# Attention stacks filled during the q, k, v stage of a transformer layer on one Trainium2 core

## What is computed

```
x = x + 0.5 * ffn(layernorm(x))
x = x + attn(layernorm(x))          # recurrent, 2 heads of 64
x = x + 0.5 * ffn(layernorm(x))

def ffn(x):                          # 16 heads of 8 channels, 8 experts
    x = x + msa(layernorm(x, ln1))
    return x + moe(layernorm(x, ln2))

def msa(x):
    q, k, v = split(x @ w_qkv)       # per batch and head: 512 x 8 each
    attn = softmax(q @ k.T / sqrt(8))
    return (attn @ v) @ w_proj
```

## Time and profile before

| | us |
|---|---|
| median of the timed runs (3) | 1562.1 |
| lowest and highest of them | 1561.02, 1567.3 |
| the profiled execution | 1553.92 |
| its span | 1552.0 |

### The profile page before, as it was taken

One profiled execution on the slowest core, in us unless ns is written; L12 is line 12 of the kernel. 1 busy time (PEld: TensorE's weight loads), 2 busy tenths in 40 slices (PEclk: granted clock), 3 DMA queues, 4 the chain that ended last, 5 costly groups with the idle time before them and its releaser, 6 DMA issues. The chain is left out here.

```text
span 1552.0 us, 39914 instructions
## 1 busy us (share of the span) xinstructions
PE 1284.2 (83%) x12720; PEld 729.3 (47%) x12721; DVE 1082.9 (70%) x1864; ACT 859.3 (55%) x1750; POOL 659.1 (42%) x767
## 2 busy tenths in 40 slices
PE   5499999999978595288789747499999999976693
PEld 3244444444368595135445444234444444376693
DVE  8588888888555233668788758688888888464232
ACT  3178888888831352234334414178888888820451
POOL 4323333333337463355566533323333333337462
PEclk9689999999975797589899958599999999965797
DMA  5513342221001222000000004311111111001124
GB/s 181 152 37 82 91 108 57 54 52 47 16 1 42 60 67 64 14 2 2 3 3 2 3 1 190 83 43 51 48 50 47 50 48 51 7 1 59 53 69 119
DMA packets 81640, 81.93 MB, mean 53 GB/s; under 512 B 16265, under 2 KB 53868, under 8 KB 81536
## 3 DMA queue, kind: packets, MB, share of 16 engines
q1 hardware_dynamic: 72704, 70.01, 16.3%
q0 software_dynamic: 4608, 8.44, 1.6%
q10 hardware_dynamic: 4224, 2.10, 0.5%
HBM read 50.56 MB, written 29.93 MB: 52 GB/s over the span
## 5 line engine op out<-in xcount | busy, mean ns | idle before, releaser
L817 DVE TENSOR_REDUCE maxima<-ps 128x2 f32<-128x1024 f32 x512 | 624.2, 1226 | 91.0 <-PE ps L646 86.4
L799 ACT ACTIVATE probs<-ps 128x512 f32<-128x512 f32 x1024 | 553.2, 593 | 90.4 <-PE ps L673 73.1
L646 PE MATMUL ps<-k_stack,q_stack 62*128 62x512 f32 x1024 | 387.6, 478 | 35.6 <-DMA k_stack<-k_split 24.4
L673 PE MATMUL ps<-q_stack,k_stack 64*128 64x512 f32 x1024 | 392.1, 461 | 0.4
L683 PE MATMUL ps<-probs,v_stack 128*32 128x256 f32 x4096 | 329.0, 393 | 1.1 <-ACT probs L799 1.0
L612 POOL TENSOR_TENSOR inv<-o_rows,minus_one 128x16 f32<-128x16 f32 x64 | 186.0, 2906 | 237.5 <-ACT o_rows L780 237.5
L646 PEld LDWEIGHTS ps<-k_stack,q_stack 62*128 62x128 f32 x1024 | 158.7, 194 | 229.9 <-issue 116.5
L673 PEld LDWEIGHTS ps<-q_stack,k_stack 64*128 64x128 f32 x1024 | 160.1, 187 | 17.0 <-issue 6.8
L683 PEld LDWEIGHTS ps<-probs,v_stack 128*32 128x32 f32 x4096 | 81.1, 108 | 172.6 <-issue 113.1
L1297 POOL DMA_INDIRECT expert_out<-yt,number x80 | 78.3, 979 | 68.1 <-POOL number L1293 34.2
L1274 DVE COPY w_now<-w 128x512 f32 x80 | 34.3, 429 | 85.9 <-issue 42.8
(11 more groups left out here) (205 smaller groups left out, 1765.5 us busy)
## 6 DMA issues: line engine op xcount, KB each, us to landing
q_stack<-q_split SPq DMA_DIRECT2D x256, 64.0 KB
k_stack<-k_split SPq DMA_DIRECT2D x512, 32.0 KB
q_split<-q_parts SPq DMA_DIRECT2D x16, 512.0 KB, 2.7
k_split<-k_parts SPq DMA_DIRECT2D x16, 512.0 KB, 3.4
xt<-sorted SPq DMA_DIRECT2D x80, 64.5 KB
w<-in_L_ffn_w SPq DMA_DIRECT2D x16, 256.0 KB, 3.1
rows<-expert_out SPq DMA_DIRECT2D x16, 256.0 KB, 3.3
x_all<-in_L_attn_x SPq DMA_DIRECT2D x8, 256.0 KB, 3.1
```

Source lines behind the costliest of these rows:

```text
L646: mm = t.matmul(psS[:, h, :], qs[g][score_rows(h), h // 2, u * P:(u + 1) * P], ks[g][score_rows(h), h // 2, :], start=True, stop=True)
L673: t.matmul(ring("e", u, n), ks[g][half(h), h // 2, u * P:(u + 1) * P], qs[g][half(h), h // 2, :], start=True, stop=True).then_inc(e_ready, 1)
L799: a.activation(probs[u % 2][:, h, :], ring("e", u, n), ACT.Exp, scale=float(DK) ** -0.5).then_inc(e_read, 1)
L817: v.tensor_reduce(maxima[i][:, :, pair, u:u + 1], psS[:, 2 * pair:2 * pair + 2, :], AX_X, ALU.max, negate=True).then_inc(s_read, 1)
```

## The change

The stacks, their semaphores, `load_group` and the constants move from the attention stage into a class `Stacks`, made before both stages, so their memory and semaphores exist in the q, k, v stage too. In that stage

- GpSimd's steps are all unrolled, and in steps 2 to 5, behind the power of that slice and once it is complete, it sets the constants of group j - 2: two blocks in `q`, two in `k`, waits until they are complete, then `v` whole, and waits again. VectorE sets none any more.
- SyncE issues the loads of group 0, 1, 2 and 3 of batch 0 in steps 4, 5, 8 and 9, each behind the two stores of its step, after a wait for the stores of slice 0 (`stored[k][0]` at 16).

In the attention stage TensorE waits once for all constants, the loads of batch 0 and the memsets of the stacks are gone, and GpSimd only sets the two small tiles before it copies v.

```diff
+class Stacks:
...
+    def load_group(self, sp, b, g):
+        def rows(dram, first, count, e):
+            heads = dram.rearrange("c (n p e) t -> c n p e t", p=PAIRS, e=2)
+            return heads[first:first + count, g, :, e, ds(b * T, T)]
+
+        for e in range(2):
+            for a in range(SPLITS):
+                row = HALF * e + a * SPLITS * DK
+                sp.dma_start(self.q[g][row:row + SPLITS * DK, :, :].bitcast(F32),
+                             rows(self.qd, 0, SPLITS * DK, e)).then_inc(self.loaded[g], 16)
+                for at in (row, row + DK):
+                    sp.dma_start(self.k[g][at:at + DK, :, :].bitcast(F32),
+                                 rows(self.kd, a * DK, DK, e)).then_inc(self.loaded[g], 16)
+
+    def set_constants(self, pool, g_, i):
+
+        for e in range(2):
+            g_.memset(self.q[i][HALF * e + ROWS:HALF * e + MAXROW, :, :].bitcast(F32), 0.0).then_inc(self.constants_set, 1)
+            g_.memset(self.k[i][HALF * e + ROWS:HALF * e + STACK, :, :].bitcast(F32), 1.0).then_inc(self.constants_set, 1)
+        pool.wait_ge(self.constants_set, 5 * i + 4)
+        g_.memset(self.v[i][:], 0.0).then_inc(self.constants_set, 1)
+        pool.wait_ge(self.constants_set, 5 * i + 5)
...
+        FIRST_LOADS = (4, 5, 8, 9)
...
+                    if isinstance(j, int) and j in FIRST_LOADS:
+                        for k in "qk":
+                            sp.wait_ge(stored[k][0], 16)
+                        stacks.load_group(sp, 0, FIRST_LOADS.index(j))
...
+                    if 2 <= j < 2 + NG:
+                        pool.wait_ge(scales_made, j + 1)
+                        stacks.set_constants(pool, g, j - 2)
...
-                pipeline(pool, SL, 0, step)
+                for j in range(SL):
+                    step(j, j % 2, lambda k: True)
...
-                for g in range(NG):
-                    load_group(0, g)
                 place(0, 0, 1)
...
-                for i in range(NG):
-                    for e in range(2):
-                        g_.memset(qs[i][HALF * e + ROWS:HALF * e + MAXROW, :, :].bitcast(F32), 0.0).then_inc(q_set, 1)
-                for i in range(2, NG):
-                    for e in range(2):
-                        g_.memset(ks[i][HALF * e + ROWS:HALF * e + STACK, :, :].bitcast(F32), 1.0).then_inc(q_set, 1)
-                pool.wait_ge(q_set, 3 * NG)
-                for i in range(NG):
-                    g_.memset(vs[i][:], 0.0).then_inc(v_set, 1)
+                pool.wait_ge(stacks.constants_set, 5 * NG)
...
+                pe.wait_ge(stacks.constants_set, 5 * NG)
                 for i in range(2):
-                    pe.wait_ge(k_set, 2 * (i + 1))
-                    pe.wait_ge(q_set, 2 * (i + 1))
                     pe.wait_ge(loaded[i], PER_LOAD)
...
-                for i in range(2):
-                    for e in range(2):
-                        v.memset(ks[i][HALF * e + ROWS:HALF * e + STACK, :, :].bitcast(F32), 1.0).then_inc(k_set, 1)
```

More of the change, by code:

```diff
@@ L21 @@
 NG = H // GROUP
+PAIRS = GROUP // 2
 F32R = mybir.dt.float32r
@@ L287, in load_constants, with __init__, sb, qkv_phase @@
     return s, load_rest, load_late, wait_rest
-def qkv_phase(nc, ps, s, x_all, z_all, v_all, qd, kd, load=None):
+class Stacks:
+    def __init__(self, nc, ctx, semaphores, qd, kd):
+        def sb(name, shape, dt=F32):
+            return ctx.enter_context(nc.sbuf_tensor(own(nc, name), shape, dt))
+        self.q = [sb(f"q_stack{i}", [P, PAIRS, T], F32R) for i in range(NG)]
+        self.k = [sb(f"k_stack{i}", [P, PAIRS, T], F32R) for i in range(NG)]
+        self.v = [sb(f"v_stack{i}", [P, TPB, GROUP, VW]) for i in range(NG)]
+        self.loaded = [semaphores(own(nc, f"stack_loaded{i}")) for i in range(NG)]
+        self.constants_set = semaphores(own(nc, "constants_set"))
+        self.qd, self.kd = qd, kd
+    def load_group(self, sp, b, g):
[17 more added lines that the diff above has]
+        pool.wait_ge(self.constants_set, 5 * i + 5)
+def qkv_phase(nc, ps, s, x_all, z_all, v_all, qd, kd, stacks, load=None):
     with Phase(nc) as ctx:
@@ L455, in _, with attention_phase @@
                 pipeline(pe, SL, 3, step)
-def attention_phase(nc, ps, s, v_all, y_all, qd, kd, load=None):
+def attention_phase(nc, ps, s, v_all, y_all, stacks, load=None):
     with Phase(nc) as ctx:
@@ L468, in sem @@
             return ctx.semaphore(name)
[L470 to L473, removed]
+        qs, ks, vs, loaded = stacks.q, stacks.k, stacks.v, stacks.loaded
         probs = [sb(f"probs{i}", [P, GROUP, T]) for i in range(2)]
@@ L482, in attention_phase @@
         minus_one = sb("minus_one", [P, TPB, GROUP])
-        k_set, q_set, v_set = sem("k_set"), sem("q_set"), sem("v_set")
-        loaded = [sem(f"stack_loaded{i}") for i in range(NG)]
+        v_set = sem("v_set")
         pool_passed, pe_passed = sem("pool_passed"), sem("pe_passed")
@@ L565, in step @@
                         sp.wait_ge(e_ready, GROUP * TPB * (G + 1))
-                        load_group(b + 1, g)
-                for g in range(NG):
-                    load_group(0, g)
+                        stacks.load_group(sp, b + 1, g)
                 place(0, 0, 1)
@@ L616, in normalize @@
                         inv[:].unsqueeze(3).broadcast_to([P, TPB, GROUP, DK]), ALU.mult).then_inc(o_done, 1)
-                pool.wait_ge(v_set, NG + 2)
+                pool.wait_ge(v_set, 2)
                 for g in range(NG):
@@ L705, in _ @@
                     if i == 0:
-                        pe.wait_ge(v_set, NG + 2)
+                        pe.wait_ge(v_set, 2)
                         turn_max(1)
-                pe.wait_ge(q_set, 3 * NG)
                 def step(b, g, first, last):
@@ L1991, in ffn @@
                 v_all = inner.enter_context(nc.sbuf_tensor(own(nc, "v_all"), [P, NT, H, DK + 1], F32))
-                qkv_phase(nc, ps, s, x_all, z_all, v_all, qd, kd, load)
-                attention_phase(nc, ps, s, v_all, y_all, qd, kd, load)
+                stacks = Stacks(nc, inner, ctx.semaphore, qd, kd)
+                qkv_phase(nc, ps, s, x_all, z_all, v_all, qd, kd, stacks, load)
+                attention_phase(nc, ps, s, v_all, y_all, stacks, load)
             project_phase(nc, ps, s, x_all, z_all, rows, expert, first_row, xs)
```

## The result

The changed kernel took 1572.5 us in the median of eight runs, the kernel before 1562.6 in eight runs on the same chip. The ratio is 1.0057, with a 95% interval of 1.0034 to 1.0080: some 9 us slower. Two later runs of the changed kernel, on two other chips, gave 1.0086 (1.0059 to 1.0113) and 1.0081 (1.0059 to 1.0102), about 13 us. The forecast was +10.9.

A forecast was written before the change was run, and what follows sets the result against it. The q, k, v stage was bound by its chain ending in SyncE's stores, the first score by loads. Per half 9.6 + 2.96 lost, in all 25.1 - 14.2 = +10.9: 1562.1 + 10.9 = 1573.0 us, range 1560 to 1581.

The forecast's parts named there:

- norm(6): VectorE's norm on slice 6 in the q, k, v stage; forecast 9.6 us late, 6.0 without blocking.
- low(5): VectorE's low-part subtractions on slice 5 in the q, k, v stage; ended 7.39 us before the last k store's issue.
- SyncE, low(5) to last k store: Loads of groups 2 and 3 in the drain, 4.3 us each, delay the last k store by 2.96 us per half.
- The gain: Attention stage: the first score needs only the stage's start, 0.30 us, gaining 7.17 us in the first half, 7.06 in the second.
- GpSimd sets the pace: q, k, v stage: GpSimd's step becomes 6.4 us against VectorE's 4.57 for four steps, making VectorE 6.0 us late.
- The set without blocking: One group's constants on GpSimd behind the power in steps 2 to 5, q, k, v stage; taken as 4.65 us.
- Blocking: q, k, v stage: memsets hold up VectorE's norms, steps take about 6.84 us, 9.6 us late instead of 6.0.
- rival 1: GpSimd sets the pace in the q, k, v stage but nothing blocks; +3.7 us, chance 0.27.
- The landing: End of the q, k, v stage: wait for the last store to land, 3.4 us in the median; no lengthening added.
- rival 3: Beyond the forecast, loads pile up behind stores or TensorE's slower clock reaches the chain's end; +15 to +19 us, chance 0.10.
- The cover: q, k, v stage: several us cover ScalarE's store waits for groups 0 and 1; 6 us cover TensorE's slower clock.

The follow-up runs named there:

- constants_only: The changed kernel with the constants still set early but the loads back in the attention stage; ratio to the kernel before 1.0058.
- pow_instead: The kernel before with three more small-tile powers per step on GpSimd in steps 2 to 5, as long as a set of constants; ratio 1.0042.
- loads_only: The changed kernel with the loads still early but the constants back in the attention stage; ratio to the kernel before 1.0061.
- late_loads: The changed kernel with the loads of groups 2 and 3 moved to the start of the attention stage; ratio to the kernel before 0.9971.
- half_sets: The changed kernel with half a group's constants behind each of the eight powers, loads as changed; ratio to the kernel before 1.0045.
- probe: A stage in front of the kernel before: twelve VectorE instructions per kind beside six GpSimd memsets, the first twelve alone; not timed against the kernel before.
- spread: As tuned, but group 0's twelve loads issued three at a time behind the stores of steps 4 to 7; ratio to the kernel before 0.9915.
- tuned: The changed kernel with half a group's constants behind each power from slice 2, only group 0 loaded early, at step 8; ratio to the kernel before 0.9953.

## Why the prediction was right, and where it was so by luck

The total was right: +10.9 forecast, +9 to +13 measured. Per half it had 5.4 us, and 6.7 came. The last k store came 12.47 us later, forecast 12.5. But two of the terms behind that were wrong by 3 us each, in opposite directions, and a third was missing; that they nearly cancel is luck. What VectorE loses was 9.6 us in the forecast and 6.5 in the run, what SyncE adds 3.0 and 5.9. For the first half:

| term | forecast | measured | shown by |
|---|---|---|---|
| first score behind stage start | 0.30, a gain of 7.17 | 0.21, a gain of 7.26 | the timeline after; constants_only (no gain) |
| pace of GpSimd, norm(6) late | 6.0 without blocking | about 4.3 | pow_instead |
| blocking | 3.6 on top | about 2.2 | the rest of low(5)'s 6.52 |
| SyncE, low(5) to last k store | 2.96 | 5.92 | timeline after; loads_only 5.62 |
| landing of the last store, longer by | 0 | 1.45 | timeline after; loads_only 1.32, late_loads 0.16 |
| sum | +5.4 | +6.63 | the first score |

**The gain** was right to 0.1 us. I had asked that TensorE find everything ready, and it did.

**GpSimd sets the pace** was right, but by another route. A step is 6.35 us, where the working had 6.4 unblocked and 6.84 blocked. The set without blocking was taken too long: 4.65 us, with memsets 1.00 us apart as in the attention stage, while in the q, k, v stage, where nothing blocks them, they come 0.90 apart (29.58 and 30.48 in half_sets), which makes about 4.2. And I expected VectorE to wait for the scales before norms 3 to 6; there is no such wait, the scales lie ready. What ties VectorE to GpSimd is the blocking itself: each norm is through right behind the set (the next instruction starts at 31.74, the set ends at 31.68), and GpSimd, which never waits in those steps, goes on at once with the next power.

**Blocking** was the right mechanism at the wrong size. The failed step is "0.2 us for a TENSOR_SCALAR let in between two memsets", that is one per memset. Two get in, so a norm of eight is through after four memsets. The first blocked norm takes 3.27 us (15.79 to 19.06), where the working had 4.9 (15.71 to 20.6); the later ones take 3.83 instead of 4.3. GpSimd's memsets of 0.94 us become up to 1.09. Against pow_instead the blocking costs 1.2 us in the first step and 0.35 in each of the three behind it (6.35 against 6.00), though each norm is 1.78 us longer: most of that takes the place of a wait of 1.3 us that rival 1 has in any case. norm(6) starts at 40.60, where the working said 43.6 blocked and 40.0 unblocked.

The Trainium skill, "SBUF — State Buffer", section "Who interferes with whom", gave the kinds: instructions in a mode that uses both ports are excluded by a GpSimd instruction, one with two SBUF inputs only by one that reads. The probe agrees with both halves: 6.25 against 3.17 us for the TENSOR_SCALAR, and 2.51 us for twelve TENSOR_TENSORs beside memsets, 0.21 each. That the two exclude each other for the whole length of an instruction, as the prediction quotes it, doesn't fit GpSimd's power: it lasts 1.64 us in pow_instead, and the norm beside it keeps its 0.34 us each. What the blocking costs could be had only from a run.

**SyncE** was mis-sized. The failed step is the group at 4.3 us, a little under its time in the quiet start of the attention stage (4.45). Directly behind two stores of 512 KB the first three transfers take 0.61 and 1.39 us instead of 0.32 and 0.65, and a group 5.63 (47.68 to 53.31) and 5.35 us (54.68 to 60.03). My own upper bound had been 5.3 for such a pile-up. The stores behind a group are slow as well, 0.76 us instead of 0.37. Of the 2.96 us that the sum is short here, the two groups make 2.4 and the stores between them 0.5.

**The landing** was not in the sum at all. I had let the last store land as before, 4.15 us behind its issue. Behind a group of loads it takes 5.60 and 5.80 in the two halves (5.47 and 5.31 in loads_only), without one 4.15 to 4.49 (before, constants_only, late_loads, spread). It isn't the loads alone, though: in pow_instead it is 5.06 and 4.61 without any, where the last four stores stand closer. What counts seems to be how much the queue holds. Loads piling up behind stores was rival 3's mechanism, and it was there: the two terms are 4.4 us per half over the forecast's. What kept the total near the forecast is that VectorE loses less than forecast, by pace and blocking together.

**The cover** that I named for the other engines held only at the end. ScalarE waited for stores to land (3.67 us before its copy at 43.85), and TensorE's granted clock fell to 0.92, but the last subtraction ends at 55.66, 4.8 us before SyncE's last issue at 60.48. The clock and those waits cost nothing in the changed kernel. In loads_only, where no memset delays the stage, the same waits cost 1.6 to 2.1 us of low(5). And with the loads out of the drain this chain is what ends last: in the first half of constants_only, from 45 to 50 us, the mean granted clock is 0.72, so part of that time went at 1.2 GHz instead of 2.4, and four matrix products (L488) take 2.73 us; in late_loads, at 1.00 there, the same four take 1.98, and the last k store is issued 1.56 us earlier (53.71 against 55.27) with low(5) the same.

Open remains why constants_only is 5 us faster than its first scores say. Its first exponents are as late as its first scores (7.1 and 6.9 us), so it is not won back before them.

## What to carry to other kernels

Work that is moved ahead into a stage is paid by that stage's slowest chain; where it drains through one queue, every transfer put there delays the last store twice, by its issue and by how the store then lands. Move only what the first instruction behind the barrier waits for (here 12 of 48 loads), in pieces that fit into each step's slack, and well before the drain. Then look at what becomes the next wait: with the loads early and the constants left behind, the first exponents waited for the constants. And when two engines slow each other, ask first whether one of them would have waited in that time anyway: only the excess counts.

## What the runs showed of the hardware

Beside back-to-back memsets of 1024 elements on GpSimd, VectorE's TENSOR_SCALAR from SBUF to SBUF goes at half its rate (0.52 us each instead of 0.26), two per memset, and the memset grows from 0.90 to 1.02 us of pitch. A COPY takes 0.52 us there too, and lengthens the memsets as much. The memsets are not lengthened by a TENSOR_SCALAR that reads PSUM, by statistics, or by a TENSOR_TENSOR of two SBUF tiles, and the statistics take 0.20 us each, as in the kernel before.

A GpSimd power over 128x8 elements takes 1.64 to 1.8 us and does not block the norm beside it (0.34 us each in pow_instead and half_sets), so the length of a GpSimd instruction is not what decides. Whether it is the number of elements or the kind of instruction was not tried.

A store of 512 KB is issued in 0.37 us, and the next stage starts 4.15 us behind it when the queue is quiet (up to 4.49 in other runs); issue takes 1.13 us and the rest 6.68 when four such stores follow twelve small loads at once (tuned, first half).
